# Who issues the store of the B and C rows: ScalarE's queue or SyncE's, in a kernel of four image layers

## The reference

```
x = x + conv3x3(gn(x))                                # layer 0
x = x + vision_mamba(gn(x))                           # layer 1
x = x + coordinate_attention_with_two_mambas(gn(x))   # layer 2
x = x + quantum_circuit_of_4_qubits(gn(x))            # layer 3
```

```
dbl = uc @ x_proj_w.T          # splits into dtr (8), B (16), C (16), one row of B and C for each state
dt  = softplus(dtr @ dt_proj_w.T + dt_proj_b)
h   = exp(dt * A) * h + (dt * u) * B[n]      # a scan over the 1024 tokens, one for each state n
y   = y + h * C[n]                           # summed over the 16 states
```

## Time and profile before

| | |
|---|---|
| median of 3 runs | 13848.69 us (13842.84 to 13849.67) |
| the profiled execution's own time | 13849.67 us |
| its span | 13847.1 us |
| POOL, DVE, PE, ACT busy | 94%, 90%, 86%, 81% |
| DMA queue of SP (q1) | 539970 packets, 3040.98 MB |
| DMA queue of ACT (q10) | 4096 packets, 16.25 MB (the 128 stores) |

### The profile page before, as it was taken

One profiled execution on the slowest core, in us unless ns is written; L12 is line 12 of the kernel. 1 busy time (PEld: TensorE's weight loads), 2 busy tenths in 40 slices (PEclk: granted clock), 3 DMA queues, 4 the chain that ended last, 5 costly groups with the idle time before them and its releaser, 6 DMA issues.

```text
span 13847.1 us, 179633 instructions
## 1 busy us (share of the span) xinstructions
PE 11911.7 (86%) x67100; PEld 8298.6 (60%) x67100; DVE 12414.4 (90%) x8118; ACT 11208.7 (81%) x16951; POOL 13046.6 (94%) x3978
## 2 busy tenths in 40 slices
PE   7888888888888888888888888888888888888886
PEld 4566666656666666666666666666666666666654
DVE  6899999999999999999999999999999999999986
ACT  5788888888888888888888888888888888888874
POOL 6899999999999999999999999999999999999995
PEclk8899999999999999999999999999999999999997
DMA  4556556656566565666655665656665555656553
GB/s 172 209 225 230 219 225 226 233 226 225 220 228 232 223 232 218 227 226 232 226 225 221 227 233 223 230 219 228 226 231 226 224 223 226 234 222 229 220 222 119
DMA packets 544936, 3068.71 MB, mean 222 GB/s; under 512 B 60378, under 2 KB 60474, under 8 KB 281794
## 3 DMA queue, kind: packets, MB, share of 16 engines
q1 hardware_dynamic: 539970, 3040.98, 58.3%
q10 hardware_dynamic: 4096, 16.25, 0.3%
HBM read 2990.40 MB, written 49.81 MB: 220 GB/s over the span
## 4 chain that ended last, share of the span: by engine, by line
POOL 30%; PE 26%; DVE 21%; issue 19%; ACT 4%; POOLq 0%; DMA 0%; DVEq 0%; SPq 0%; ACTq 0%
POOL ring L1055 24%; DVE ring L1546 14%; PE y_acc L1582 11%; PE work L1567 10%; POOL ring L1047 6%; DVE slot L1529 4%; PE y_acc L1567 2%; PE slot L1582 1%; PE work L1582 1%; PE slot L1567 1%; ACT ring L1238 1%; ACT L1080 1%; ACT padded L1186 1%; DVE du L1365 0%; ACT slot L1238 0%
## 5 line engine op out<-in xcount | busy, mean ns | idle before, releaser
L1055 POOL TENSOR_TENSOR ring<-ring,c_rows 128x2048 f32<-128x2048 f32 x2048 | 9278.2, 4543 | 303.9 <-DVE ring L1546 294.5
L1546 DVE TENSOR_TENSOR_SCAN ring<-ring,slot 128x1024 f32<-128x1024 f32 x2560 | 5805.1, 2279 | 249.9 <-PE slot L1582 142.3
L1582 PE MATMUL y_acc<-wk,ring 128*128 128x128 f32 x32768 | 4510.7, 290 | 913.1 <-POOL ring L1055 900.9
L1582 PEld LDWEIGHTS y_acc<-wk,ring 128*128 128x128 f32 x32768 | 3998.4, 150 | 1741.4 <-POOL ring L1055 1332.5
L1047 POOL TENSOR_TENSOR ring<-du,b_rows 128x1024 f32<-128x1024 f32 x1536 | 3627.5, 2369 | 313.2 <-PE y_acc L1582 205.1
L1546 DVE TENSOR_TENSOR_SCAN ring<-slot,ring 128x1024 f32<-128x1024 f32 x1536 | 3473.6, 2273 | 322.9 <-POOL ring L1047 234.6
L1238 ACT ACTIVATE ring<-dt,a_neg 128x1024 f32<-128x1024 f32 x2560 | 2865.3, 1141 | 82.9 <-PE y_acc L1582 67.6
L1529 DVE TENSOR_TENSOR slot<-du,slot 128x1024 f32<-128x1024 f32 x1824 | 2205.5, 1214 | 262.6 <-PE slot L1567 254.4
L1238 ACT ACTIVATE slot<-dt,a_neg 128x1024 f32<-128x1024 f32 x1536 | 1709.1, 1114 | 700.5 <-DVE ring L1546 690.9
L1567 PE MATMUL work<-h_new,fused 128*128 128x512 f32 x4096 | 1996.9, 608 | 90.2 <-DVE du L1365 64.0
L1080 ACT ACT_TABLE_LOAD x1555 | 1995.1, 1283 | 28.7
(11 more groups left out here) (177 smaller groups left out, 9290.4 us busy)
## 6 DMA issues: line engine op xcount, KB each, us to landing
c_rows<-cb_rows_scratch SPq DMA_DIRECT2D x2048, 1024.0 KB, 4.7
b_rows<-cb_rows_scratch SPq DMA_DIRECT2D x1536, 512.0 KB, 6.2
x_next<-in_x SPq DMA_DIRECT2D x32, 512.0 KB, 5.7
x_new_scratch<-x_next SPq DMA_DIRECT2D x32, 512.0 KB, 6.8
h_old<-h_new SPq DMA_DIRECT2D x32, 512.0 KB, 6.9
x_old<-x_new_scratch SPq DMA_DIRECT2D x32, 512.0 KB, 5.5
out<-x_old SPq DMA_DIRECT2D x32, 512.0 KB, 6.9
cb_rows_scratch<-stack ACTq DMA_DIRECT2D x128, 124.0 KB
```

The costliest lines, as they stand in the source:

```text
L1055: pool.tensor_tensor(pair, pair, c_rows[:, k % CB_BUFS, :, :], ALU.mult).then_inc(prod_ready, 1)
L1546: dve.tensor_tensor_scan(slot, a, b, 0.0, MUL, ADD).then_inc(scan_done, 1)
L1582: ins = pe.matmul(chunk(out_t, j), chunk(x, j), kc("ident"), is_transpose=True, start=start and j % (BANK // P) == 0, stop=stop, skip_grou ...
```

## The change

The store of the rows is no longer issued by ACT after the second copy, but by SP, at fixed places of its queue: `store_rows(d, base, rows_done)` waits until ACT has made the copies and issues the DMA. In an image the store of direction 2 stands ahead of the loads of pair 32, that of direction 3 ahead of those of pair 40, that of direction 0 of the next image behind the loads of pair 63 and ahead of those of the next image's pair 0, and that of direction 1 behind the next image's pair 3. In the set-up both stand likewise around the loads of pairs 0 to 3. The plans get three more names that a first copy must come after: ("kron", 2, 2) in the set-up, ("scan", 60) for direction 3 and ("scan", 123) for direction 1.

```diff
--- before.py
+++ after.py
@@ -627,6 +627,8 @@
     f = held_back(f[:h1], ("zero",)) + held_back(f[h1:], ("bn_shift", "bn1"))
     o = held_back(o, ("fuse", 1, TAPS - 1)) + gate_z(0, 0) + conv(1, 0) + conv(1, 1)
     o += project(1)
+    rows = [x[0] for x in o].index(("cb_rows", 1, 0))
+    o = o[:rows] + held_back(o[rows:], ("kron", 2, 2))
     t = held_back(t, ("a_neg2",), ("diag", HALVES - 1), ("dtw", 2 * PARTS - 1))
     return best_plan([f + o, t] + set_up(), "begin", PACES)
 
@@ -653,9 +655,13 @@
         turn = [x[0] for x in steps].index(("turn_b", d))
         return steps[:turn] + held_back(steps[turn:], *[("zmul", u, 1) for u in zs[-1:]])
 
+    def rows_after(steps, d, *after):
+        k = [x[0] for x in steps].index(("cb_rows", d, 0))
+        return steps[:k] + held_back(steps[k:], *after)
+
     ops = gate_z(0, 1, [] if first else [("take", "before")]) + conv_after(2, 0) + conv_after(3, 0) + conv_after(2, 1)
     ops += project_after(2) + gate_z(1, 0, [("take", 1)]) + conv_after(3, 1)
-    ops += project_after(3, over(2)) + gate_z(1, 1, [("take", 3)])
+    ops += rows_after(project_after(3, over(2)), 3, ("scan", 4 * NST - 4)) + gate_z(1, 1, [("take", 3)])
     dts = []
     for p in range(1, PASSES):
         d, h = parts_of(p)
@@ -668,7 +674,7 @@
             + held_back(f[n:], ("conv_in", 3, 1, TAPS - 1, 1), ("z", 1, 1, 1))
         ops += held_back(conv_after(0, 0), ("h1", 1)) + conv_after(1, 0) + conv_after(0, 1) + project_after(0, over(3))
         ops += gate_z(0, 0, [("take", 5)]) + conv_after(1, 1)
-        ops += project_after(1, over(6))
+        ops += rows_after(project_after(1, over(6)), 1, ("scan", UNITS - 5))
         dts += held_back(timestep(0, 0), over(6)) + turn_du(0, 0, last_z(UNITS))
         streams += [f]
     if not first:
@@ -936,6 +942,11 @@
                 sp.dma_start(lay[:, c * AMPS:(c + 1) * AMPS], k1).then_inc(matrices_in, 16)
                 sp.dma_start(lay[:, (2 + c) * AMPS:(3 + c) * AMPS], k2).then_inc(matrices_in, 16)
 
+            def store_rows(d, base, rows_done):
+
+                sp.wait_ge(*done(base, rows_done))
+                sp.dma_start(cb_dram[d].rearrange("(n t) -> n t", t=TOK), cb_rows).then_inc(cb_out, 16)
+
             def load_pair(k, s):
 
                 (d, h, _), i, b = unit_of(2 * k), k % (NST // 2), k % CB_BUFS
@@ -959,6 +970,7 @@
 
             for last_use in (("postw_mask", CH - 1), ("mixw_copy", 1, HALVES - 1), ("fuse", 1, TAPS - 1), ("dtw", 2 * PARTS - 1)):
                 sp.wait_ge(*done(NONE, before_n[last_use]))
+            store_rows(0, NONE, before_n[("cb_rows", 0, 1)])
             for k in range(CB_BUFS):
                 load_pair(k, 0)
             sp.dma_start(x_new, x_next[:, :]).then_inc(x_moved, 16)
@@ -966,7 +978,11 @@
             def image(kind, s):
                 base = bases(kind, s)
                 of = plan_n[kind]
+                store_rows(1, base, ("A", 0))
                 for k in range(CB_BUFS, PAIRS):
+                    for d in (2, 3):
+                        if 2 * k == NST * pass_of(d, 0):
+                            store_rows(d, base, of[("cb_rows", d, 1)])
                     if k == LOAD_AT and kind != "last":
                         sp.wait_ge(x_moved, 16 * s + 16)
                         sp.dma_start(x_next[:, :], x_in[s + 1]).then_inc(x_loaded, 16)
@@ -989,6 +1005,7 @@
                         sp.dma_start(x_new, x_next[:, :]).then_inc(x_moved, 16)
                     load_pair(k, s)
                 if kind != "last":
+                    store_rows(0, base, of[("cb_rows", 0, 1)])
                     for k in range(CB_BUFS):
                         load_pair(k, s + 1)
 
@@ -1204,17 +1221,11 @@
                     ins = act.activation(t1[:, 0:256], w[:, 0:256], ACT.Square)
                 ins.then_inc(side["A"], 1)
 
-            def store_rows(d, rows_done):
-                act.wait_ge(*rows_done)
-                act.dma_start(cb_dram[d].rearrange("(n t) -> n t", t=TOK), cb_rows).then_inc(cb_out, 16)
-
             for name, e, bank, after in before:
                 if e == "A":
                     ready_table(name)
                     hold(act, "A", NONE, before_n, after)
                     step(name, 0, bank_of[bank])
-                    if name[0] == "cb_rows" and name[2] == 1:
-                        store_rows(name[1], done(NONE, before_n[name]))
             want(HOME)
 
             def image(kind, s):
@@ -1245,8 +1256,6 @@
                         ready_table(name)
                         hold(act, "A", base, of, after)
                         step(name, image_of(name, s), bank_of[bank])
-                        if name[0] == "cb_rows" and name[2] == 1:
-                            store_rows(name[1], done(base, of[name]))
                 want(HOME)
 
             each_image(act, image)
```

## The result

The changed kernel took 14048.55 us (median of 4 runs, 14037.55 to 14055.0) against 13849.18 us: a ratio of 1.0144, 95% interval 1.0126 to 1.0162. It is 199 us slower, where 141 us had been forecast (13990, with 13930 to 14050 for 8 in 10). The profiled execution has a span of 14041.2 us.

A forecast was written before the change was run, and what follows sets the result against it. The prediction took GpSimd (POOL), busy 94% of the span, to bound the kernel. 13848.7 + 144 (30 boundaries of 4.8 us) - 3 for ACT's gain = 13990 us, 1.0% slower; 13930 to 14050 for 8 in 10.

The forecast's parts named there:

- The mechanism: At each image boundary ACT's direction 1 copy waits for direction 0's store to land, stalling ACT 5.4 us.
- the prediction's last paragraph: Expected signs: some 5 us idle before ACT's direction 1 copy only, scan 125 equally late, POOL's busy time unchanged.
- The landing: Direction 0's store on SP's queue lands 10.0 us after pair 63's load is issued, bounds 7.8 to 13.3.
- a ring worked off in order: SP's queue finishes the load, then the store: 4.2 + 5.0 + 0.3, so landing after 9.5 us.
- the like case on two queues: A store beside a c_rows load on another queue, engines taking turns: SP went on 10.8 us after the load's issue.
- the low value: Landing of 9.5 us behind pair 63's load, with 4.2 us of it for the load itself.
- the formula: Delay at one image boundary is landing minus 5.2 us; bounds of the landing give 2.6 to 8.1 us.
- The sum: Delays added up at one boundary: next image starts 4.8 us late, takes as long as before; 30 x 4.8 = 144 us.
- the 3 us allowed for ACT's gain: Saving from ACT no longer issuing stores, outside the boundary's 0.25 us: 3 us in all, range 0 to 25.
- The image period of 428: Sign in the profile after: middle images repeat every 428 us; 423 us would prove the prediction wrong.
- The first rival: Direction 1's store also delays unit 9's b_rows load; if it missed by 2 us, 60 us more: 14050; chance 8%.
- The quick store: Rival: SP's store runs over all engines, landing by 5.2 us without delay; around 13838 us (13824 to 13846); chance 6%.

The follow-up runs named there:

- run 3: Against the kernel before: only direction 0's store on SP, at the changed kernel's place, directions 1, 2 and 3 issued by ACT; 14052.59 us (1.0147).
- run 4: Against the kernel before: direction 0's store issued by ACT, directions 1, 2 and 3 by SP at the changed kernel's places; 13848.74 us (0.9999).
- run 8: Changed kernel plus 22 unread matmuls on PE per middle image, ahead of the matmul that waits for ACT's stall; 14012.76 us (1.0116).
- run 1: Changed kernel, but in middle images SP issues direction 0's store ahead of the loads of pair 63, one product earlier; 13854.53 us (1.0004).
- run 5: Changed kernel with each store issued as two DMAs of 16 and 15 rows at the same places of SP's queue; 13858.09 us (1.0005).
- run 2: Changed kernel, but in middle images SP issues direction 0's store ahead of the loads of pair 62, two products earlier; 13849.49 us (1.0001).
- run 9: SP's stores split in two, direction 0's ahead of pair 62: 13849.4 us (1.0); split alone on the kernel before: 13833.16 us, again 13836.19 us.
- run 6: Changed kernel, but in the middle plan ACT's waiting copy and the bank's last copy stand behind decay 127; 13994.38 us (1.0105).

## Why the prediction came out as it did

- **The mechanism was right.** Direction 0's store behind the load of pair 63 makes ACT wait at the copy of direction 1 in 30 images, and nowhere else (runs 3 and 4). The copy's idle time, the late scan 125, the unchanged busy times and the missing cost of the other stores came as the prediction's last paragraph had them.
- **The landing was taken too early.** I took 10.0 us behind the load, between 9.5 for a ring worked off in order and 10.8 for the like case on two queues. In the median image ACT's copy started 10.65 us behind the load, which with the prediction's 0.1 for the hop puts the landing at 10.55. The load itself landed after 5.6 us in the boundary shown, not the 4.2 that the low value stood on. From 4837.6 to 4842.5, behind the load's last packets, the queue shows the store alone (packets, MB, share of 16 engines):

```profile
q1 hardware_dynamic: 33, 0.13, 6.3%
```

6.3% is one engine of 16, busy throughout. So the ring in order is what happened, only with a slower load: 5.3 us to the load's last packet, 4.8 for the store's, 0.4 until SP's next load goes out. The like case on two queues was no turn-taking either: from 4634.3 to 4639.2 the store's 32 packets there also followed the load's. By the formula, landing less 5.2, this is 5.35 us an image in place of 4.8: 17 us over 30 images.

- **The clock was left out.** The sum let PE be as quick after the stall as before it. It was not: 36 us in run 8. From one load of pair 63 to the next the middle images took 423.25 us before, 429.8 after and 428.6 with PE kept busy, each the mean of 29. Together 144 + 17 + 36 = 197, against 199 us measured; the 3 us allowed for ACT's gain did not come. The image period of 428, by which the prediction wanted to be judged, was 429.8 for these reasons.
- **The image behind the boundary is not rigid, and some of this agreement is luck.** The sum lets the next image "take as long as before". The starts of POOL's products, counted from the load of pair 63 (medians of 29 boundaries), say otherwise. In run 8 the product of pair 63 is 5.5 us late, as the formula has it, and that of pair 1 6.2 us. But the images then take about 426.7 us (11 of 29) or about 430.0 us (15 of 29), 3.4 or 6.8 us more than before; that the mean, 5.3, lies near the formula is chance. In the changed kernel pair 1's product is 7.8 us late, and the images take about 429.0 or 431.2 us (12 of 29 each). So the clock costs 1.6 us at the boundary (7.8 less 6.2), and 1.2 us of it are left at the end of a mean image. In run 1 it is 0.9 us at pair 63 and 0.3 at the end. What decides between the two lengths is open.
- **A slip in the range.** By the prediction's own sum a landing of 10.8 gives 13848.7 + 168 - 3 = 14014 us, not 14020. Nothing hangs on it, and the measured 14048.55 lies 1.5 us inside the upper end of the range for 8 in 10, which had been widened for other reasons than the clock. That it lies inside is luck too.
- **The first rival did not come.** The b_rows load behind direction 1's store landed after 11.4 us instead of 8.2, at about 4871.0, and its input started at 4876.03, 5 us later. POOL was at pair 1, itself late from the stall, until 4876.06, so nothing waited for that load.
- **The quick store was a matter of the rows.** The rival had SP's queue spread the 31 rows. The queue did not; two DMAs of 16 and 15 rows did (run 5), with a landing at 5.1 us where the rival had worked out 5.2, and all but 8 us of the loss gone.
- **The gain of ACT was nothing.** 3 us had been allowed for it; runs 2, 4 and 9 show none.

Left open: a second staging buffer, which should take the wait away without moving anything, was not tried. Why the load of pair 63 lands later with the store behind it (5.6 us against 4.2) was not looked into.

## What to carry to other kernels

Before a DMA is moved to another queue, ask who waits for its landing, and take the time from what stands ahead of it in the new queue: here one buffer's reuse hung on it, and 6 us at one place in an image cost more than 128 issues taken from a busy engine could have given back. Moving a wait along an engine's queue does not free what the waiting instruction holds; look for its PSUM bank too. And a stall that leaves TensorE without work can cost a second time, at half the clock: here after 5.78 us without work, and after 3.68 us in run 6.

## What was not expected of the hardware

A store of 31 rows and 124 KB lands 10.5 us behind a 1 MB load in the same queue, while 16 and 15 rows land 5.1 us behind it. And PE's matmuls took 1.97 us in place of 1.04 to 1.09 after 5.78 us without work, with a granted clock of 0.50; 4.92 us of matmuls whose results nobody reads, in that gap, kept it at 1.00 and made the kernel 36 us faster. The same stall in every image gave images of two lengths, 3.4 us apart in run 8.
